# Two-layer graph and expert network: a second tile in 64 of the merged stage fetched row by row, by SyncE and ScalarE

## The reference, cut to what matters

```python
x_proj = (x @ W).reshape(n, H, D)                  # attention, 8 heads of 32
e = alpha_src[row] + alpha_dst[col]
e_exp = jnp.exp(e - m[col])
att = e_exp / (segment_sum(e_exp, col) + 1e-16)
x = x + segment_sum(att[:, :, None] * x_proj[row], col)
h = relu(bn(einsum('bfd,edh->bfeh', layernorm(x), W1) + b1))   # 8 experts
h = relu(bn(einsum('bfeh,ehk->bfek', h, W2) + b2))
y = einsum('bfeh,ehd->bfed', h, Wo) + bo
x = x + einsum('bfed,fe->bfd', y, w)
```

## Time and profile before

| | |
|---|---|
| median of 3 runs | 7003.0 us (6998.93 to 7009.14) |
| the profiled execution's own time | 7016.87 us |
| its span, first to last instruction | 7015.1 us |
| mean granted TensorE clock | 0.739 |
| merged stage, first gather to the end | 3942 to 7015 us |
| one loop body of four batches in it | 118.3 us, mean of 22 |
| POOL busy over the span | 3105.2 us (44%) |
| PE busy over the span | 4354.6 us (62%) |
| ACT busy over the span | 1057.7 us (15%) |

### The profile page before, as it was taken

One profiled execution on the slowest core, in us unless ns is written; L12 is line 12 of the kernel. 1 busy time (PEld: TensorE's weight loads), 2 busy tenths in 40 slices (PEclk: granted clock), 3 DMA queues, 4 the chain that ended last, 5 costly groups with the idle time before them and its releaser, 6 DMA issues. The chain is left out here.

```text
span 7015.1 us, 90314 instructions
## 1 busy us (share of the span) xinstructions
PE 4354.6 (62%) x20634; PEld 3735.3 (53%) x20634; DVE 2028.4 (29%) x8126; ACT 1057.7 (15%) x2222; POOL 3105.2 (44%) x3258
## 2 busy tenths in 40 slices
PE   3545545545454554544499547777777777777778
PEld 2544444445444443544488436565665656566566
DVE  4322322222232222222256412222222222222222
ACT  2000000000000000000156201111111111111112
POOL 4544444443444444344212445555554545555541
PEclk5666666666666666666699768888888888888889
DMA  5222222222222222222111323333333333333321
GB/s 153 80 72 76 70 70 69 74 76 64 75 71 70 69 73 75 65 75 72 50 64 50 112 76 88 83 86 84 87 82 85 83 86 85 84 86 85 85 82 43
DMA packets 257609, 546.82 MB, mean 78 GB/s; under 512 B 70050, under 2 KB 126758, under 8 KB 257292
## 3 DMA queue, kind: packets, MB, share of 16 engines
q0 software_dynamic: 151888, 420.85, 21.4%
q10 hardware_dynamic: 54206, 68.04, 3.0%
q1 hardware_dynamic: 51198, 55.05, 2.6%
HBM read 482.52 MB, written 61.15 MB: 77 GB/s over the span
## 5 line engine op out<-in xcount | busy, mean ns | idle before, releaser
L742 POOL DMA_INDIRECT ring<-xn,index x1540 | 1457.3, 946 | 1879.1 <-ACT index L755 1421.0
L1812 POOL DMA_INDIRECT ring<-table,index x1591 | 1517.2, 954 | 1465.1 <-ACT index L1828 1006.3
L911 PE MATMUL bank<-spare,ring 128*128 128x64 f32 x6448 | 939.8, 311 | 1015.6 <-DMA ring<-xn 671.5
L911 PEld LDWEIGHTS bank<-spare,ring 128*128 128x128 f32 x6448 | 926.4, 230 | 970.5 <-DMA ring<-xn 657.4
L2005 PE MATMUL bank<-ring,acc 128*128 128x264 f32 x3232 | 932.2, 426 | 394.4 <-issue 310.6
L2005 PEld LDWEIGHTS bank<-ring,acc 128*128 128x128 f32 x3232 | 664.7, 209 | 580.3 <-issue 387.4
L1878 ACT ACTIVATE ework<-bank,bn 128x256 f32<-128x256 f32 x800 | 402.8, 560 | 2316.4 <-remote 1077.4
L1014 DVE TENSOR_TENSOR spare<-spare,bank 128x128 f32 x800 | 230.3, 288 | 1520.9 <-PE bank L911 811.4
L2245 DVE SCALAR_TENSOR_TENSOR y<-bank,gate,y 128x256 f32 (+1 forms) x400 | 175.1, 479 | 1511.7 <-remote 1443.0
L2021 PE MATMUL bank<-acc,wa 128*128 (+1 forms) x1600 | 437.2, 401 | 211.9 <-issue 209.1
L926 PE MATMUL bank<-wblk,cells 128*128 128x128 f32 x1632 | 355.1, 387 | 326.4 <-issue 326.4
(11 more groups left out here) (265 smaller groups left out, 2933.1 us busy)
## 6 DMA issues: line engine op xcount, KB each, us to landing
ring<-xn SPq DMA_DIRECT2D x4224, 1.0 KB
ring<-table SPq DMA_DIRECT2D x3200, 1.0 KB
ring<-xn ACTq DMA_DIRECT2D x1920, 1.0 KB
ring<-table,index POOLq DMA_INDIRECT x1591
ring<-xn,index POOLq DMA_INDIRECT x1564
sums<-acc ACTq DMA_DIRECT2D x101, 132.0 KB
sums<-spare ACTq DMA_DIRECT2D x101, 128.0 KB
acc<-sums ACTq DMA_DIRECT2D x25, 264.0 KB
```

Source lines behind the costliest of these rows:

```text
L742: pool.indirect_dma_start(ring[:, m * BT + t, :], None, k.xn_d, bass.IndirectOffsetOnAxis(ap=index[m][:, t:t + 1], axis=0)).then_inc(got[m ...
L911: ins = pe.matmul(win[q][:, t, h * CELLS:(h + 1) * CELLS], ring[:, m * BT + q * QUAD + t, h * P:(h + 1) * P], onehot[:, q * QUAD + t, :], ...
L1812: pool.indirect_dma_start(ring[:, par * BT + t, :], None, k.table1_d, bass.IndirectOffsetOnAxis(ap=index[par][:, t:t + 1], axis=0)).then_i ...
```

## The change

In each loop body of the merged stage the last tile of the batch with m = 1 isn't gathered by GpSimd either. Its 128 rows go singly to a new slot, `2 * BT + 1`. Rows 80 to 127 (48) are issued by SyncE, ahead of its 128 rows for m = 3; rows 0 to 79 (80) by ScalarE in five groups of 16: after `relu(2)` of u = 0 and of u = 1 in the periods with m = 2 and m = 3, and after `relu(2)` of u = 0 in the period with m = 0. Each group loads 16 addresses into registers and issues 16 DMAs. The addresses come by one small DMA that ScalarE issues in the period with m = 1. ScalarE and TensorE wait for the new tile on two new semaphores. The first loop body (n = 0) gathers this tile as before. The last gather fetches 12 tiles in place of 16, and TensorE multiplies 12. The last body of each loop is written out, so that it can leave out the groups that have no next tile. The other path of the stage (`general`, not taken with these inputs) gets the same rows.

```diff
+ODD_ROWS1 = 80
@@ rounds
-    with eng.Fori(0, ROUNDS - 2) as i:
+    with eng.Fori(0, ROUNDS - 3) as i:
         iteration(i + 2, True, True, gathers)
+    iteration(ROUNDS - 1, True, True, gathers)
@@ gnn1_ffn1
-        ring = a.sb("ring1", [P, 2 * BT + 1, ROW1])
+        ring = a.sb("ring1", [P, 2 * BT + 2, ROW1])
...
         def tile_at(par, m, t):
-            return 2 * BT if m == 3 and t == BT - 1 else par * BT + t
+            return 2 * BT + (m == 1) if par == 1 and t == BT - 1 else par * BT + t
+
+        def odd_first(n):
+            return (BT * (4 * n + 1) + BT - 1) * P
...
             elif m == 1:
-                eng.wait_ge(got[par * BT + t], 16 * n + 16 + had[par * BT + t])
+                eng.wait_ge(got[par * BT + t], 16 + had[par * BT + t])
+                eng.wait_ge(odd_rows, 16 * (P - ODD_ROWS1) * n + 1)
+                eng.wait_ge(odd_act_rows, 16 * ODD_ROWS1 * n + 1)
@@ SyncE: rows
-                sp.wait_ge(places_read, 16 * n + 16)
+                if not first:
+                    sp.dma_start(odd_sp[:], k.place1_d[cols(odd_first(n) + ODD_ROWS1, P - ODD_ROWS1)].rearrange(
+                        "(a e) -> a e", a=1)).then_inc(places_read, 16)
+                sp.wait_ge(places_read, 32 * n + 16)
                 past_waits(sp, k)
-                if not (isinstance(n, int) and n == 0):
+                if not first:
+                    sp.wait_ge(done, 4 * n - 2)
+                    past_waits(sp, k)
+                    for c in range(0, P - ODD_ROWS1, BT):
+                        sixteen(odd_sp, c, ODD_ROWS1 + c, 2 * BT + 1, odd_rows)
                     sp.wait_ge(done, 4 * n)
                     past_waits(sp, k)
                 for c in range(0, P, BT):
+                    sixteen(places, c, c, 2 * BT, rowed)
@@ GpSimd
-                for m in range(3):
-                    gather(4 * n + m, m % 2, BT)
-                gather(4 * n + 3, 1, BT - 1)
-            gather(BATCHES - 1, 0, BT)
+                for m in range(4):
+                    gather(4 * n + m, m % 2, m, BT - m % 2)
+            gather(BATCHES - 1, 0, 0, LAST_TILES)
@@ ScalarE
+            def odd_sixteen(n, c):
+                if c == 0:
+                    act.wait_ge(odd_act_read, 16 * n)
+                    past_waits(act, k)
+                _, place = nc.values_load_multi_w_load_instructions(
+                    odd_act[0:1, c:c + BT], engines=[act.engine], min_val=0, max_val=(N - 1) * ROW1_BYTES,
+                    skip_runtime_bounds_check_because="a source is a node's number")
+                for e in range(BT):
+                    act.dma_start(ring[c + e:c + e + 1, 2 * BT + 1, :].bitcast(U8),
+                                  bytes_d[:, cols(place[e], ROW1_BYTES)]).then_inc(odd_act_rows, 16)
+
+            def some_rows(m, n, u):
+                if m >= 2 and not (isinstance(n, int) and n + 1 >= BATCHES // 4):
+                    odd_sixteen(n + 1, (2 * (m - 2) + u) * BT)
+                if m == 0 and u == 0 and not (isinstance(n, int) and (n == 0 or n >= BATCHES // 4)):
+                    odd_sixteen(n, ODD_ROWS1 - BT)
...
                     for j2, e in experts(work_of, u, LAYER2):
                         relu(2, j2, e)
+                    if gathers:
+                        some_rows(m, n, u)
+                if gathers and m == 1 and not (isinstance(n, int) and n + 1 >= BATCHES // 4):
+                    read_odd(n + 1)
```

More of the change, by code:

```diff
@@ L1594, in batch_fours1, with four @@
 def batch_fours1(eng, emit):
-    with eng.Fori(0, BATCHES // 4) as n:
+    def four(n):
         for m in range(4):
             emit(2 * n + m // 2, m % 2, m, n, BT)
+    with eng.Fori(0, BATCHES // 4 - 1) as n:
+        four(n)
+    four(BATCHES // 4 - 1)
     emit(BATCHES // 2, 0, 0, BATCHES // 4, LAST_TILES)
@@ L1780, in rows @@
                 for c in range(0, P, BT):
[L1781 to L1786, removed]
+                    sixteen(places, c, c, 2 * BT, rowed)
+            sp.sem_inc(odd_rows, 1)
             for i, n in enumerate(names):
@@ L1805, in _, with gather @@
         def _(pool):
-            def gather(b, par, tiles, first=False):
+            def gather(b, par, m, tiles):
                 pool.wait_ge(indexed, b + 1)
-                if not first:
+                if not (isinstance(b, int) and b < 2):
                     pool.wait_ge(done, b - 1)
@@ L1850, in load_sums, with read_odd @@
                 act.dma_start(xn, group_rows(k.sums_d, j)).then_inc(s_load, 16)
+            def read_odd(n):
+                act.dma_start(odd_act[:], k.place1_d[cols(odd_first(n), ODD_ROWS1)].rearrange("(a e) -> a e", a=1)
+                              ).then_inc(odd_act_read, 16)
+            def odd_sixteen(n, c):
+                if c == 0:
+                    act.wait_ge(odd_act_read, 16 * n)
+                    past_waits(act, k)
+                _, place = nc.values_load_multi_w_load_instructions(
+                    odd_act[0:1, c:c + BT], engines=[act.engine], min_val=0, max_val=(N - 1) * ROW1_BYTES,
+                    skip_runtime_bounds_check_because="a source is a node's number")
+                for e in range(BT):
+                    act.dma_start(ring[c + e:c + e + 1, 2 * BT + 1, :].bitcast(U8),
[5 more added lines that the diff above has]
+                    odd_sixteen(n, ODD_ROWS1 - BT)
             def load(j):
@@ L1928, in batch @@
                 b = 2 * i + par
-                for t in range(BT):
+                for t in range(tiles):
                     wait_rows(act, par, i, m, n, t)
@@ L1932, in batch @@
                 by_tile = alpha.rearrange("p (h t) -> p t h", h=HEADS)
-                if m == 3:
+                if par == 1:
+                    last = tile_at(par, m, BT - 1)
                     act.copy(by_tile[:, 0:BT - 1, :], ring[:, BT:2 * BT - 1, D:ROW1])
-                    act.copy(by_tile[:, BT - 1:BT, :], ring[:, 2 * BT:2 * BT + 1, D:ROW1]).then_inc(alpha_c, 1)
+                    act.copy(by_tile[:, BT - 1:BT, :], ring[:, last:last + 1, D:ROW1]).then_inc(alpha_c, 1)
                 else:
@@ L1948, in batch @@
                     load_starts(b + 2, par)
+                if m == 1 and not (isinstance(n, int) and n + 1 >= BATCHES // 4):
+                    act.wait_ge(done, 4 * n + 2)
+                    past_waits(act, k)
+                    read_odd(n + 1)
+                    for c in range(0, ODD_ROWS1, BT):
+                        odd_sixteen(n + 1, c)
             def narrow():
@@ L1998, in quad @@
             def quad(b, par, half, m, n, q):
+                last = isinstance(b, int) and b == BATCHES - 1
+                if last and q >= LAST_TILES // QUAD:
+                    return
                 if q == 0:
```

26 lines of the change are left out of this document (17 added, 9 removed).

## The result

The changed kernel takes 7367.56 us (median of 4 runs, 7357.84 to 7377.15) where the kernel before takes 7000.97 (median of 4, 6989.63 to 7009.14): ratio 1.0524, interval 1.0511 to 1.0536. It is slower by 367 us. The profiled execution took 7377.15 us with a span of 7374.6, 359.5 more than the span before.

The account below looks back on a forecast made before the run. The prediction took GpSimd's bursts and ScalarE's chain to the index copy, taking turns, as the bound: 7.4 + 13.0 + 0.0 = +20.4 us a body, 23 bodies +469, +5 first body, -7 end, +467; forecast 7470 us, range 7250 to 7620.

Parts of the forecast that it names:

- isn't last; its rows hide in the gaps: SyncE's 176 rows need about 126 us a body, under the 139 that ScalarE's groups make; cost taken as 0.
- A group's price, 6.7 us: One ScalarE group of 16 rows outside the slow stretch, register load included, costs 6.7 us.
- G3, +7.4: Burst in the period m = 2, both groups beside it: next burst starts at 37.9 us instead of 30.5, +7.4.
- G0, +13.0: Burst in the period m = 3, both groups beside it: next burst at 39.1 us instead of 26.1, +13.0.
- slow stretch: Part of each gather burst, from some 5 us in until it ends, in which all sequencers nearly stand.
- The alternative kept for an early relu (+10): Beside G0, `relu(2)` keeps its early place: four or five rows in the slow stretch, the rest behind; +10 us.
- rival 1: Half is hidden: only the second groups of each period count, 12.2 us a body, about 7275 us; chance 0.16.
- G1, 0.0: Burst in the period m = 0, one group: the tile's 1.25 us gain and the group's excess cancel, 0.0.
- G2, 0: Burst in the period m = 1: one small ScalarE DMA of 0.4 us, behind relus, costs 0.
- The first body, +5: First body with groups, before the experts' work has begun: ScalarE is nearly empty, so +5 us.
- rival 3: SyncE becomes the bound: +6 to +20 us a body, 7130 to 7460 us, 7300 at the middle; chance 0.13.
- The end, -7: The last gather has 4 tiles fewer, 5.0 us, and PE four tiles fewer, about 1.9 us: -7 us.

Follow-up runs that it names:

- late_moved: Changed kernel with the two groups behind `relu(2)` of u = 1 moved behind the next period's window copy; 4585.99 us, 0.9970 of the kernel before (4599).
- changed: The changed kernel itself, run on a chip where the kernel before takes 4599 us; 4900.32 us, ratio 1.0659 to the kernel before.
- late_again: late_moved once more, on a chip where the kernel before takes 6931 us; 7298.65 us, ratio 1.0529 to the kernel before.
- tile_again: tile_alone once more, on a chip where the kernel before takes 6931 us; 6867.83 us, ratio 0.9915 to the kernel before.
- act_alone: Changed kernel, but GpSimd gathers the tile, ScalarE's five groups write an unread slot, SyncE has 128 rows only; 4886.61 us, 1.0627 of the kernel before.
- sp_alone: Changed kernel, but GpSimd gathers the tile, SyncE's 48 more rows write an unread slot, ScalarE has no groups; 4594.39 us, 1.0000 of the kernel before.
- heads_again: heads once more, on a chip where the kernel before takes 6931 us; 7377.75 us, ratio 1.0646 to the kernel before.
- heads: Changed kernel with all five groups behind their periods' window copies, ahead of layer 1; 4581.67 us, 0.9960 of the kernel before (4599).
- before_here: The kernel before, unchanged, run for its trace on a chip of the 4600 us kind; 4602.3 us.
- tile_alone: Changed kernel, but from the second body on nobody fetches the m = 1 tile; 4559.92 us, 0.9923 of the kernel before (4595).

## Why the prediction was right, and where its sum was off

The forecast was 7470, range 7250 to 7620; measured 7368, or +359.5 in the profiled spans where the sum said +467.

**What bounds the kernel: right.** POOL's long waits still end at the index copy, in 88 waits, and what grew is those waits. On a chip without gaps the same change costs 301 us, so the turn-taking between GpSimd and ScalarE isn't needed for the loss. There the place ahead of the copy is: shown by late_moved against changed, where only two groups move. On the kind of chip that was forecast, the changed kernel's trace shows the same waits, but moving the groups doesn't bring the time back, since SyncE's list is nearly as long (late_again). That SyncE "isn't last; its rows hide in the gaps" held for the changed kernel, by 2 us a body and not by the 13 of 139 against 126: the address lists took 7.7 us, not 3.

**A group's price, 6.7 us: near.** Rows went at 0.33 to 0.34 us outside the slow stretch. From relu to relu it is 6.96 us, 6.0 without the 0.92 that two relus take from start to start (four in 1.93); ahead of the copy it is 7.03 less 1.93, or 5.1. The forecast let the first group end 6.8 us behind the start of its relu, which is so, and then added the relus' 1.0 to the second.

**G3, +7.4: right.** Measured +6.9 (table), the gap 18.3 us where "near 19" was forecast. The forecast was 0.7 for the first group, most of it hidden behind layer 2 of u = 1, and 6.7 for the second; late_again agrees, with G3 at +1.2 when the second is gone.

**G0, +13.0: the term that was mis-sized.** Measured +6.2. I expected SyncE's 48 more rows to lengthen G0's slow stretch and `relu(2)` to come at 22.9; it came at 8.4 in the body shown, with the gap at 11.5 us and not 19, and close to the forecast in one body of 21. The term was also taken from a body whose G0 was 26.1 us, 1.2 under the mean of 27.3. The alternative kept for an early relu (+10) put four or five rows into the slow stretch and the rest behind it; in the body shown eight rows were out ahead of it, and the eight in it took 1.2 us each, not 2.1. So nearly the whole first group fits into the burst. For G0 rival 1's account (the first group hidden, the second paid) is the true one in most bodies.

**The slow stretch.** "From some 5 us in" fits SyncE's rows and not the others. PE before, in the burst of the earlier trace rows, still has full pace until 11.3 us in, and ScalarE's group beside G0 until 12.3:

```profile
6152.98 1.24 PE L2021 MATMUL bank<-acc,wa 128*128 x5
```

**G1, 0.0: +1.5, a sum of two that don't cancel.** The tile alone takes 2.6 off (tile_again) and the group puts 4.1 back (33.6 against 29.5), the two traces being of two chips. **G2, 0: +1.2**, though nothing was put there; tile_again has it 0.9 shorter than before, so G2 inherits part of what its neighbours gain or lose.

**The first body, +5: mis-sized.** The stretch ahead of the window took +30.7, where my sum had +25.4 for it (5 and one body of 20.4), and by another cause: SyncE's list, rival 3, which in the changed kernel holds at the start alone. In the window no long wait of POOL or PE ends at SyncE's rows.

**PE's clock, 0.** The granted clock fell from 0.84 to 0.81, and PE is busy 122 us more in the window, on the chain or not: on the 4600 chip the same window has the clock at 1.00 before and 0.93 changed. No run separates what this costs.

**The end, -7: right** at -8.2, the stage's start moving by -2.8.

**The total.** It came out nearer than its terms: G0 was 6.8 us a body too high, while G1, G2 and the start were too low. The chances at its end (slower 0.90, faster 0.07) differ by 0.01 from those of the rivals that they add up.

Put together: 22 bodies at 5.0 us too much is 109, the start 5.3 too little, the end and the stage's start 4 between them: 467 - 109 + 5.3 - 4 = 359. By the table G0 is 6.8 and G3 0.5 too much, G1 and G2 together 2.7 too little.

**The rules cited.** That spreading DMAs over issuing engines saves little was right here, and the runs show more: it costs 292 us of 4595 where the issuing engine releases the others (act_alone), and some 5 on SyncE (sp_alone). The advice to issue early needs room in the whole list of the issuing engine: five groups at the heads of periods gain 0.4% on one kind of chip, and on the other SyncE's 176 rows alone take 132 to 135 us a body.

**What stays open.** The groups and SyncE's rows cost a body 17.6 to 21 us there (132.1 to 135.5 against 114.5). SyncE's list sets this in late_again and heads_again, but sp_alone and act_alone ran only on the other kind of chip, so what either part costs alone on this one, and whether fewer rows on SyncE and more at ScalarE's heads would gain, wasn't measured.

## What to carry to other kernels

Rows that an engine issues singly are paid where they stand in its list, not where it is idle by the busy count: look first for what the engine's next signal releases. Put such a block behind the signal and not ahead of it; where nothing else is near its limit this gave back 314 us of 4900. Then look again for what ends the waits: on the other kind of chip it gave nothing, because the next list, SyncE's, was 2 us a body behind. And price it on the chip where it will run: the same placement (heads) was 0.4% faster on one and 6.5% slower on another.

## What the runs showed of the hardware that was not expected

**The slow stretch shows on some chips and not on others.** One program takes 7001 and 6931 us on two, 4595 and 4599 on two others. On the latter bursts run 1.25 us a tile as well, but the other sequencers don't stand still beside them: the windows of the same 22 bodies show PE at clock 1.00 and 1748.54 us where the earlier trace rows has 2602.82:

```profile
2717.18:4465.72 1748.54, 1685.94 (x7620) 1397.54 (x7618) 627.24 (x2533) 432.65 (x1036) 1326.16 (x1387) 1.00 0.45 126
```

What differs between these chips, and whether it is the chip or its state at that time, no trace here tells.

**A gap at the back edge of ScalarE's loop.** In the changed kernel on the 4600 chip the window copy of the period m = 0 comes 3.01 us after ScalarE's last work, all of it behind the loop's branch:

```profile
3334.40 0.56 ACT L1923 ACTIVATE ework<-bank,bn 128x256 f32<-128x256 f32 x1
3337.97 0.38 ACT L1862 COPY acc<-bank 128x264 f32<-128x264 f32 x1 [3.01 <-issue]
```

The median from the branch to the next instruction is 3.2 us in changed, act_alone and late_moved, and 0.26 in before_here, sp_alone, tile_alone and heads. The Trainium skill (Runtime: NRT & Kernel Launch, Instruction fetch mechanics) says that a taken branch whose target has left the small window of loaded code stalls for a fetch. The three kernels with the gap have ScalarE's longer list, which agrees; heads has a list as long and no gap, which the rule doesn't explain, and the programs of changed and late_moved have 0.4 us there on the 7000 kind of chip. The gap isn't what the change loses by: late_moved has it and is 0.3% faster than before.
